# Attention scores of four heads from row quarters of the array, with rows of 1 MB and blocks of one query chunk

## The reference

```python
q, k, v = (x @ W.T for W in (Wq, Wk, Wv))              # 16 heads of 32
scores = einsum('bhsd,bhtd->bhst', q, k) * 32 ** -0.5
scores = where(mask, -inf, scores)
out = einsum('bhst,bhtd->bhsd', softmax(scores), v) @ Wo.T
xn = out / sqrt(mean(out * out) + 1e-6) * rms_scale
x = x + xn * (1 + sc) + shift                           # shift, sc = silu(cond) @ Wc.T + bc
x = x + hamilton(q_left, hamilton(x * gate, conj(q_right)))
```

## Time and profile before

| | |
|---|---|
| median of 3 runs | 814.6 us (812.99 to 817.53) |
| the profiled execution | 813.31 us, its span 811.5 us |
| products and loads on PE | 4864 of each |
| scores | 512 products (496 and 16), mean 452 and 460 ns |
| DMA | 216.62 MB, 267 GB/s over the span |
| granted clock of PE | 1.0 throughout (2.4 GHz) |

### The profile page before, as it was taken

One profiled execution on the slowest core, in us unless ns is written; L12 is line 12 of the kernel. 1 busy time (PEld: TensorE's weight loads), 2 busy tenths in 40 slices (PEclk: granted clock), 3 DMA queues, 4 the chain that ended last, 5 costly groups with the idle time before them and its releaser, 6 DMA issues.

```text
span 811.5 us, 16319 instructions
## 1 busy us (share of the span) xinstructions
PE 796.2 (98%) x4864; PEld 594.1 (73%) x4864; DVE 609.0 (75%) x1492; ACT 607.5 (75%) x1511; POOL 514.1 (63%) x371
## 2 busy tenths in 40 slices
PE   9999999999999899999999999999999999999987
PEld 6788888888887677677767776777677767776764
DVE  4612314213237799999999999999999999999866
ACT  6222323222326899999999999999999999999881
POOL 0899993000000011278888888888878888888894
PEclk9999999999999999999999999999999999999999
DMA  8964545546377988988999899999998999889301
GB/s 284 343 233 183 207 163 224 178 172 220 146 285 254 344 283 288 342 325 296 322 323 333 303 325 335 316 320 307 314 337 302 304 339 314 302 305 326 103 27 53
DMA packets 90575, 216.62 MB, mean 267 GB/s; under 512 B 10600, under 2 KB 11240, under 8 KB 82304
## 3 DMA queue, kind: packets, MB, share of 16 engines
q1 hardware_dynamic: 90352, 215.41, 75.8%
q10 hardware_dynamic: 144, 0.26, 0.1%
HBM read 133.81 MB, written 81.82 MB: 266 GB/s over the span
## 4 chain that ended last, share of the span: by engine, by line
PE 41%; ACT 36%; issue 9%; POOL 6%; DMA 3%; DVE 3%; SPq 1%; ACTq 0%; DVEq 0%; POOLq 0%
ACT probs L182 25%; PE banks L551 10%; PE banks L550 10%; PE banks L552 10%; ACT turned_probs L1129 7%; PE banks L889 3%; POOL late L769 3%; PE banks L924 3%; PE banks L163 3%; ACT o_T L1161 2%; DMA blocks_scratch<-staged_blocks 2%; POOL late L1267 1%; ACT inv_T L1145 1%; DMA turned_probs<-blocks_scratch 1%; PE banks L938 1%
## 5 line engine op out<-in xcount | busy, mean ns | idle before, releaser
L182 ACT ACTIVATE probs<-probs,least 128x512 f32<-128x512 f32 x512 | 393.8, 850 | 0.0
L174 DVE CUSTOM_DVE_ANT_0 probs<-banks,mask_bias 128x512 f32<-128x512 f32 x512 | 328.2, 682 | 14.5 <-PE banks L163 12.3
L889 PE MATMUL banks<-ident,probs 128*128 128x128 f32 x1568 | 230.2, 273 | 0.0
L889 PEld LDWEIGHTS banks<-ident,probs 128*128 128x128 f32 x1568 | 190.6, 140 | 42.1 <-issue 7.7
L163 PE MATMUL banks<-k_rows,q_rows 128*128 128x512 f32 x496 | 198.4, 452 | 0.2 <-issue 0.2
L1129 ACT ACTIVATE turned_probs<-banks 128x512 f32<-128x512 f32 x263 | 179.9, 712 | 8.5 <-PE banks L924 4.5
L182 ACT ACTIVATION_READ_ACCUMULATOR probs<-probs,least 128x1 f32 x512 | 168.0, 328 | 0.0
L477 DVE SCALAR_TENSOR_TENSOR late<-banks,late 128x512 fp32r<-128x512 f32 x64 | 43.9, 689 | 154.5 <-ACT late L414 154.5
L769 POOL TENSOR_TENSOR late<-rot,late 128x2048 f32<-128x2048 f32 x28 | 128.9, 4602 | 0.6 <-DVE late L1056 0.6
L414 ACT ACTIVATE late<-banks 128x512 fp32r<-128x512 f32 x64 | 38.2, 598 | 117.7 <-PE banks L552 110.6
L924 PE MATMUL banks<-turned_probs,v_sb 128*32 128x512 f32 (+1 forms) x1088 | 117.0, 570 | 6.2 <-DMA turned_probs<-blocks_scratch 4.6
(11 more groups left out here) (137 smaller groups left out, 1338.1 us busy)
## 6 DMA issues: line engine op xcount, KB each, us to landing
q_rows<-q_scratch SPq DMA_DIRECT2D x64, 512.0 KB, 6.5
k_rows<-k_scratch SPq DMA_DIRECT2D x62, 512.0 KB, 7.3
blocks_scratch<-staged_blocks SPq DMA_DIRECT2D x120, 256.0 KB, 4.6
turned_probs<-blocks_scratch SPq DMA_DIRECT2D x120, 256.0 KB, 3.5
q_scratch<-late SPq DMA_DIRECT2D x64, 256.0 KB, 2.3
k_scratch<-late SPq DMA_DIRECT2D x64, 256.0 KB, 2.3
out<-late SPq DMA_DIRECT2D x29, 256.0 KB, 4.9
raw<-in_xT SPq DMA_DIRECT2D x7, 1024.0 KB, 5.7
```

Of the source, the lines that this page charges most:

```text
L174: dve.tensor_tensor_reduce(self.probs[:, n % RING, :], self.ps[:, n % SCORE_BANKS, :], self.mask_bias[:, c, :], 1.0, 3e38, ALU.add, ALU.mi ...
L182: act.activation(self.probs[:, n % RING, :], self.probs[:, n % RING, :], ACT.Exp, bias=self.least[:, n % 32:n % 32 + 1], scale=-1.0, accum ...
L889: last = pe.transpose(turn_bank("tile", n)[:, j * P:(j + 1) * P], probs[:, n % RING, j * P:(j + 1) * P], ident[:, :])
```

## The change

**Scores** are made for four tiles at once, a score group: the four heads of one chunk. Each head's 32 dimensions lie in a quarter of the partitions, and its products contract over 32 rows, in three passes (high-high, high-low, low-high), into one bank for each head. There are four score banks, and a score group waits until the group before is masked in all four. Two turn banks are left.

**Rows** of a unit are one DMA of 1 MB, parts of q and k side by side, in three buffers; stores in `projections` join the high and low part in one DMA.

**Blocks** are now chunk 0 of all four heads, the first four tiles of a group; the last of them is turned at place 5 instead of 2. They are read back with one DMA, which waits for all four stores, into a buffer of their own (`landing`). `turned_probs` has two full buffers for the other 12 tiles, in turn by group. Value products are 16 of 384 columns and then 16 of 128 columns for the blocks.

**Order**: all tables are new. Value products stand at place 1 (before: 2), behind a score group. ACT and DVE copy 8 and 4 tiles of a group as before. POOL rotates before it splits. `probs` has 9 slots (before: 10). The modulation is finished after batch 0, and PE waits for it there. Loops are written out; q and k tasks alternate. The class `Made` (not shown) would move work of later units into `projections`; with `MADE = 30` it applies to no unit.

```diff
-RING, SLOTS = 10, HG + 1
-SCORE_AHEAD, MASK_AHEAD, EXP_AHEAD = 7, 5, 2
-SCORE_BANKS, TURN_BANKS = 3, 3
-BLOCKS_AT = (1, 2, 2, 3)
+RING, SLOTS = 9, 3
+GROUP_AHEAD, MASK_AHEAD, EXP_AHEAD = 2, 6, 4
+SCORE_BANKS, TURN_BANKS = HG, 2
+BLOCKS_AT = {"first": (), "early": (1, 1, 3, 5), "whole": (1, 1, 3, 5)}
...
-VALUES_AT = {"first": 2, "early": 2, "whole": 2, "half0": 3, "half1": 2, "half2": 2, "half3": 2}
+VALUES_AT = {"first": 11, "early": 1, "whole": 1, "half0": 2, "half1": 2, "half2": 2, "half3": 3}
...
-         "whole": (1, 2, 1, 0, 1, 0, 0, 3, 1, 1, 1, 0, 2, 0, 2, 1),
+          "whole": (1, 0, 0, 0, 0, 1, 0, 0, 0, 1, 0, 0, 0, 1, 0, 0),
...
-         "whole": (2, 3, 0, 0, 1, 1, 0, 2, 1, 2, 0, 1, 0, 1, 1, 1),
+         "whole": (2, 0, 0, 1, 0, 3, 1, 2, 0, 1, 2, 0, 2, 0, 0, 2),
...
+    def load(self, sp, u):
+        sp.dma_start(f32(self.parts[:, self.slot(u)]), self.scr["rows"][u]).then_inc(self.landed[self.slot(u)], 16)
+
+    def head(self, u, part, i):
+        return self.parts[i * D:(i + 1) * D, self.slot(u), part]
+
+def score_products(pe, banks, q, k, t):
+    for way, (q_part, k_part) in enumerate(((0, 0), (0, 1), (1, 0))):
+        for i in range(HG):
+            last = pe.matmul(banks[:, i, :], q(q_part, i)[:, t], k(k_part, i), start=(way == 0), stop=(way == 2))
+    return last
...
-        if n >= SCORE_BANKS:
-            pe.wait_ge(self.masked, n - SCORE_BANKS + 1)
-        pe.matmul(self.ps[:, n % SCORE_BANKS, :], self.rows.q[:, u % 2, i, c * P:(c + 1) * P], self.rows.k_of(u)[:, i, :],
-                  start=True, stop=True).then_inc(self.scored, 1)
+        if group > 0:
+            pe.wait_ge(self.masked, HG * group)
+        score_products(pe, self.ps, lambda part, i: self.rows.head(u, part, i),
+                       lambda part, i: self.rows.head(u, 2 + part, i),
+                       slice(c * P, (c + 1) * P)).then_inc(self.scored, 1)
...
     def load(self, sp, v):
-        for a in (0, 2, 1, 3):
+        for a in range(TC):
             sp.wait_ge(self.out[a], 16 * (v + 1))
-            sp.dma_start(self.turned_probs[:, HG * v % SLOTS, a, :], self.scr[v % 2, a]).then_inc(self.moved, 16)
+        sp.dma_start(self.landing[:, v % 2], self.scr[v % 2].rearrange("a p t -> p a t")).then_inc(self.moved[v % 2], 16)
...
+                    last = pe.matmul(value_ps[i * D:(i + 1) * D, span(chunks[1:] if whole else chunks)], weights,
+                                     turned_probs[:, v % 2, 0:len(chunks) - whole, i, part, :],
                                      start=(part == 0), stop=(part == TC - 1))
+                if part == TC - 1 and whole:
+                    for j in range(TC):
+                        for i in range(HG):
+                            h = HG * g + i
+                            last = pe.matmul(value_ps[i * D:(i + 1) * D, 0:P].rearrange("p (a t) -> p a t", a=TC),
+                                             v_sb[:, b % 2, j, h * D:(h + 1) * D],
+                                             blocks.landing[:, v % 2].rearrange("p a (j i t) -> p j i a t", j=TC, i=HG)[:, j, i],
+                                             start=(j == 0), stop=(j == TC - 1))
...
+            pe.wait_ge(mod_ready, 1)
+            for b in range(1, B - 1):
+                batch(b, b % 2)
...
                 if NG < v <= POOL_GROUPS:
                     add(v - NG - 1)
+                if NG < v <= POOL_GROUPS:
+                    rotate(v - NG - 1)
                 if 0 < v <= POOL_GROUPS:
                     split(v - 1)
                 if v <= POOL_GROUPS:
                     if v > NG:
-                        rotate(v - NG - 1)
+                        rotation_sums(v - NG - 1)
```

## The result

The changed kernel takes 858.25 us (median of 4 runs, 855.49 to 860.55) against 814.57 for the kernel before, measured beside it: ratio 1.053, interval 1.0482 to 1.0579. It is slower, by 43.7 us where 14.5 were forecast.

A forecast was written before the change was run, and what follows sets the result against it. PE, DVE and ACT were all taken as full at 16.1 to 16.3 us a group; PE's grew 0.51 to 16.75, +14.5 us over 28.5 groups. With edges cancelling, 813.3 + 14.5 gave 827.8 profiled, median 829, range 806 to 872.

The forecast's parts named there:

- three full engines: Attention groups: PE, DVE and ACT each need 16.1 to 16.3 us, so relieving one gains nothing and loading one costs.
- PE's own work: Score groups on PE by row quarters with shape changes: four take 4.08 us against 3.76, +0.32 a group.
- the saved change: A score group directly before the value products saves one change of the array's shape on PE: -0.2 us a group.
- The banks: Four score banks refilled at once and two turn banks make PE and DVE wait: +0.15 us a group, ends 0 and 0.6.
- The edges: Outside the steady groups: modulation +3.6 us, first group -2.4 and POOL's end -1.2 cancel to 0.
- Modulation: After the first batch PE waits for DVE to finish the modulation: +3.6 us, ends 2.3 and 4.5.
- First group: PE's 2.37 us stand for the first blocks at attention's start goes: -2.4 us, ends -2.4 and +3.
- The end: Last 75 us: POOL rotates before splitting and no longer stands for the norm: -1.2 us, ends 0 and -8.
- 1: Score groups: the shape change hides or costs little, ACT's 16.17 us a group binds, median 814.6; chance 0.22.
- 4: Rival 1's claim holds and POOL's chain at the end loses its stands too, -8 us: median 807; chance 0.14.
- 2 (blocks' chain): Blocks' stores and load bind before value products: group 17.2 us or more, median 843 or 863; chance 0.14.
- 3 (quarters in sequence): Score groups: row quarters or their weight loads run one after another, PE 19.5 us a group, median 907; chance 0.08.

The follow-up runs named there:

- e1_serial: The changed kernel with each score group as four products over 128 rows, its one wait and one signal kept: 866.7 us.
- e2_ring: The changed kernel with four products over 128 rows per score group, each bank waited for and signalled by itself: 843.3 us.

## Why the prediction was right or wrong, point by point

**The direction and the reading of three full engines were right.** A change that loads PE or makes engines wait is paid 28 times: 1.06 us a group made 29.6 of the 42.2 us.

**PE's own work: +0.32 forecast, about 0 measured.** With 1.05 us of standing in 17.28, PE has 16.2 us to do, as before. The score groups were well put: 16.23 less 3.59 for the value products, 5.72 for thirteen turns and 2.82 for the projection leaves 4.10 for four of them, where I had 4.08. Too dear were the value products. They last 3.59 and lasted 3.57:

```profile
588.04 0.51 PE L163 MATMUL banks<-k_rows,q_rows 128*128 128x512 f32 x1
```

(584.47 to 588.04; the earlier trace rows doesn't show this score, and I had put the next one at 588.15). So cutting them into long and short blocks cost nothing where I took 0.2. And the two scores before them took 0.77 (583.70 to 584.47) where two take 0.47, while the score group before them now takes 0.90 as it does before a turn: the saved change is worth 0.30, where I took 0.2. That is +0.34, 0 and -0.30 for the +0.32, +0.2 and -0.2 of the forecast.

**The banks: the step that failed.** "I take 0.15 a group (ends 0 and 0.6, one DVE operation)." It measured 1.05, seven times that and past its upper end, and it is the whole growth of the group: PE stood 0.66 for masks and 0.39 for a turn bank. The runs divide it so: banks freed at once cost 0.77 to 0.9 a group (e1_serial to e2_ring); without that wait 0.5 to 0.6 are left over the kernel before, 0.46 of them PE's stand for a turn bank; whether it comes of there being two or of the new order, no run with that order tells, since it has no third bank to give. In the order of the kernel before, two turn banks alone are 1.06. These prices don't add up to the 1.06 of the change. As I read it, a wait at one door hides part of a wait at the other; no run shows that by itself.

The error in the step was its form. I compared DVE's cover (two operations, 1.22 us) with PE's score group (1.02) "and two signals" and found them level. The cycle should have been added up: answer 1.21, four masks 2.45, signal 0.23, that is 3.89 for four tiles against 16.22/4 = 4.06 available. It looks as if it fits. But one of the four rounds is 5.51 long because the value products stand in it, so the other three had 16.22 - 5.51 = 10.7 us, 3.57 each, and they need 3.8 to 4.1. All numbers for that but the signals stood in the rows of before: 3.98 of value products, 1.02, a turn, four masks at 0.61.

The Trainium skill, "TensorEngine Tiling (Array Packing)", Gotcha 1: PSUM Pressure, says that row tiles write to different banks and that software has to synchronise; the runs agree, and the price was there, not in the array: the banks cost a group 1.05 us, the row quarters themselves gained 0.3 (17.60 to 17.28).

**The edges don't cancel.** Forecast 0, measured +12.6. *Modulation*: +3.6 forecast. PE stands 2.45 us, and then its granted clock is down:

```profile
41.18 0.19 PE L703 MATMUL banks<-nan_part,ones 128*8 128x1 f32 x2
43.82 0.79 PE L655 MATMUL banks<-v_sb,o_hi 128*128 128x512 f32 x1 [2.45 <-DVE mod L617]
44.41 0.63 PE L656 MATMUL banks<-mod_b,o_hi 128*128 128x512 f32 x1
44.84 0.63 PE L657 MATMUL banks<-v_sb,o_lo 128*128 128x512 f32 x1
```

From 43.8 to 46 us the granted clock is 0.50, the lower of the two levels (1.2 GHz), and products stand 0.43 us apart instead of 0.227. Wait and slow products make 3.9 us, as the run without the wait shows up to 265.50; of its gain 2.6 reach the value products, since that run lost 1.5 to another stretch at the lower clock. The size is within the ends, but partly by luck: of the two mechanisms I had named one, and its 3.6 measured 2.45. DVE was done when I had said, but PE ran to 41.37 (the first line) and not to 40.27. *Spacing*: 8 batches of 96 products by 0.0065 is 5.0 us, in no view that I had. "Loops written out ... 0" and "rows stores ... 0" were the nearest statements; the stores are cleared, the loops hardly come into question, since the first batch is in no loop in either kernel. *First group*: -2.4 forecast, with +3 as the far end. The wait of the earlier trace rows is gone, but others took its place, for the most part at the same two doors as in the steady stretch:

```profile
269.66 0.97 PE L150 MATMUL banks<-row_parts 32*128 32x512 f32 x12 [2.85 <-DVE least L184]
275.73 0.63 PE L994 MATMUL banks<-ident,probs 128*128 128x128 f32 x4 [0.18 <-ACT probs L190]
277.70 0.63 PE L994 MATMUL banks<-ident,probs 128*128 128x128 f32 x4 [1.12 <-ACT turned_probs L1240]
```

The three make 4.15; with its two short ones (0.29 at 262.53, 0.25 at 263.96) the kernel before had 2.91, so +1.2. Modulation, spacing and this make 3.9 + 5.0 + 1.2 of the 11.7; the rest isn't taken apart. *The end*: +0.9, forecast -1.2. One wait for the last rows of 1 MB is new:

```profile
789.60 0.97 PE L150 MATMUL banks<-row_parts 32*128 32x512 f32 x12 [1.37 <-DMA row_parts<-rows_scratch]
```

so "nobody waits for rows now, so 0" holds for the steady stretch and not at the end. What POOL's new order gained or didn't there, no run takes apart.

**The rivals.** 1 and 4 (no cost, faster): no; the banks cost. 2 (blocks' chain): the measured group of 17.28 is what it would give, and it isn't the cause. Stores landed in 3.5 us and the one load in 5.6, where the earlier trace rows gave 4.6 and 5.7, and in its profile PE never stands for the landing in the steady stretch. It isn't far off: one load is issued at 591.81 and, at 5.6, lands 1.4 us ahead of the value products of 598.83. In the ring and in several other runs single groups did wait for it. A distance alone doesn't tell rivals apart; the releaser does. 3 (quarters in sequence): no; 12 loads take 0.54 us beside the streams:

```profile
563.38 0.54 PEld L150 LDWEIGHTS banks<-row_parts 32*128 32x128 f32 x12 [0.66 <-DVE least L184]
```

**The transfers** were right in the steady stretch: the DMA share fell from 0.94 to 0.69, and PE waits for no rows there.

## What to carry to other kernels

Before banks are freed in one go, add up the whole cycle between producer and consumer (answer, all consumers' operations, signal), set it against the time that is left for that turn once the long block of other work has had its own, and not against the mean. A buffer taken from one ring to enlarge another has to be priced by itself: in the order of the kernel before, the bank given up is worth all that the groups lost. And where work and waits alternate, taking work from the busiest engine, 96% on the page, gives back only the part that lies inside the cycle.

## What the runs showed of the hardware

- Products of 32 rows in four row quarters really run together: 12 of 512 columns in 0.90 us, four in 0.45. Beyond their streams (0.64 and 0.213) that is 0.24 to 0.26 for leaving the shape, and the turn ahead of them takes 0.53, where it takes 0.44 before another turn and 0.35 before a long product, so 0.09 to 0.18 for entering it.
- From the start of a score group of 0.90 us to the consumer's first mask 1.21 us pass; with one pass of three DVE shows no standing before its masks in 400 to 600 us.
- PE idle for 2.45 us was followed by about 3 us at the lower clock level, products 0.43 us apart. A stand of 2.82 us had the same sequel in one run, one of 2.85 at the same place of the kernel after had not. The four executions of the kernel after go with their clock: they took 855.5 and 856.5 us at a mean granted clock of 0.997 and 0.998, and 860.0 and 860.6 at 0.992 and 0.991.
- The same 96 products a batch stood 0.2267 us apart in one kernel and 0.233 in another at full granted clock. Moving operands by 2,112 bytes, cutting the stores, another column order of the weights and the DMA scratch size were not the cause; it isn't known.
